# Masking the attention scores on VectorE and taking the exponential on ScalarE in eight pieces with a bias, with the feed-forward loads split up, in a six-layer local-attention megakernel

## The reference

```python
for i in range(DEPTH):                       # 6 layers
    x = attn_layer(shift_tokens(x), Wqkv[i], q_scale[i], k_scale[i], Wo[i]) + x
    x = ffn_layer(shift_tokens(x), ln_g[i], ln_b[i], W1[i], b1[i], W2[i], b2[i]) + x
# local_attention: 16 heads of 64, windows of 32 queries that see 64 keys
    mask = (it < jb) | (it > jb + w) | (jb == -1)
    sim = jnp.einsum('bhwie,bhwje->bhwij', bq, bk2) * QK_SCALE
    sim = jnp.where(mask, -jnp.finfo(sim.dtype).max, sim)
    attn = jax.nn.softmax(sim, -1)
    out = jnp.einsum('bhwij,bhwje->bhwie', attn, bv2)
# ffn_layer: layer norm with gain g and shift bln, then
    hg = xn @ W1 + b1
    a, gate = jnp.split(hg, 2, -1)
    return a * jax.nn.gelu(gate, approximate=False) @ W2 + b2
```

## Time and profile before

| | |
|---|---|
| time, median of 3 runs | 1740.41 us (1739.14 to 1745.62) |
| the profiled execution's own time | 1741.98 us |
| its span in the trace | 1740.2 us |
| mean granted clock of TensorE | 0.985 |
| busy, PE / PEld | 1666.1 us (96%) / 1210.5 us (70%) |
| busy, DVE | 1381.5 us (79%) |
| busy, POOL | 1187.3 us (68%) |
| busy, ACT | 1092.9 us (63%) |

### The profile page before, as it was taken

One profiled execution on the slowest core, in us unless ns is written; L12 is line 12 of the kernel. 1 busy time (PEld: TensorE's weight loads), 2 busy tenths in 40 slices (PEclk: granted clock), 3 DMA queues, 4 the chain that ended last, 5 costly groups with the idle time before them and its releaser, 6 DMA issues.

```text
span 1740.2 us, 74075 instructions
## 1 busy us (share of the span) xinstructions
PE 1666.1 (96%) x31420; PEld 1210.5 (70%) x31420; DVE 1381.5 (79%) x2661; ACT 1092.9 (63%) x1943; POOL 1187.3 (68%) x1163
## 2 busy tenths in 40 slices
PE   5889999999999999999999999999999999999995
PEld 2357777777777777677777677777677777677774
DVE  4688888887888888788888788888788887788863
ACT  2256666666666666566666566666666666566653
POOL 0377777776777767676776677677677777666751
PEclk9799999999999999999999999999999999999998
DMA  3032223332223323222323222333222332222222
GB/s 106 25 93 66 68 67 79 89 76 71 66 68 81 88 68 78 68 65 69 96 71 78 70 68 63 92 78 77 71 69 66 80 87 74 74 64 66 66 61 76
DMA packets 109735, 127.86 MB, mean 73 GB/s; under 512 B 52064, under 2 KB 55648, under 8 KB 109152
## 3 DMA queue, kind: packets, MB, share of 16 engines
q1 hardware_dynamic: 109408, 123.13, 27.9%
HBM read 20.27 MB, written 2.10 MB: 13 GB/s over the span
## 4 chain that ended last, share of the span: by engine, by line
PE 89%; DVE 4%; SPq 2%; ACT 2%; DMA 2%; issue 1%; POOL 0%; ACTq 0%; DVEq 0%; POOLq 0%
PE QKb L471 21%; PE O L594 11%; PE F L499 9%; PE VTb L512 9%; PE S L471 9%; PE S L529 8%; PE S L559 5%; PE F L616 4%; PE F L628 4%; PE F L629 3%; PE S L522 2%; SPq L397 1%; DVE t L823 1%; PE F L568 1%; DMA prm<-in_params 1%
## 5 line engine op out<-in xcount | busy, mean ns | idle before, releaser
L968 POOL TENSOR_TENSOR t<-t 128x512 f32<-128x512 f32 x384 | 488.7, 1273 | 306.6 <-DVE t L823 298.7
L823 DVE TENSOR_TENSOR t<-QKb,table 128x1024 f32<-128x1024 f32 x384 | 468.8, 1221 | 156.8 <-ACT sq L668 156.3
L962 POOL TENSOR_TENSOR t<-t,rn 128x512 f32<-128x512 f32 x384 | 400.5, 1043 | 136.0 <-DVE rn L863 136.0
L471 PE MATMUL QKb<-wq_sb,x_sh 128*128 128x512 f32 x768 | 426.3, 637 | 12.4 <-DVE t L823 11.7
L668 ACT ACTIVATE sq<-QKb 128x512 f32<-128x512 f32 x384 | 230.8, 601 | 321.7 <-PE QKb L471 314.7
L499 PEld LDWEIGHTS F<-wo_sb,OT 128*128 128x128 f32 x1536 | 202.9, 193 | 89.6 <-issue 88.7
L512 PEld LDWEIGHTS VTb<-cst,t 128*128 128x128 f32 x1536 | 186.6, 141 | 104.8 <-issue 94.0
L512 PE MATMUL VTb<-cst,t 128*128 128x128 f32 x1536 | 230.6, 273 | 0.6 <-POOL t L962 0.5
L594 PEld LDWEIGHTS O<-PT,V 64*64 64x64 f32 x12288 | 199.2, 135 | 42.7 <-issue 41.8
L876 DVE TENSOR_REDUCE ss<-sq 128x16 f32<-128x1024 f32 x192 | 224.4, 1169 | 0.0
L594 PE MATMUL O<-PT,V 64*64 64x32 f32 x12288 | 219.2, 221 | 0.9 <-DVE rn L863 0.5
(11 more groups left out here) (136 smaller groups left out, 2165.9 us busy)
## 6 DMA issues: line engine op xcount, KB each, us to landing
V<-v_tok SPq DMA_DIRECT2D x1440, 64.0 KB, 2.0
wq_sb<-in_wqkv SPq DMA_DIRECT2D x36, 256.0 KB, 3.7
wo_sb<-in_wo SPq DMA_DIRECT2D x6, 512.0 KB, 5.0
xs<-xm SPq DMA_DIRECT2D x48, 64.0 KB
xs<-xm SPq DMA_DIRECT2D x48, 63.5 KB
w_sb<-in_w SPq DMA_DIRECT2D x6, 341.0 KB, 3.3
w_sb<-in_w SPq DMA_DIRECT2D x6, 192.0 KB, 3.1
y_spill<-OT SPq DMA_DIRECT2D x1, 1024.0 KB, 4.1
```

The lines of the kernel that those rows point to most:

```text
L471: return pe.matmul(out_, x_sh[:, pr, P * tile:P * (tile + 1)], wq_sb[:, col:col + 512], start=True, stop=True)
L823: dve.tensor_tensor(t12[:, v, :, :].rearrange("p c (h d) -> p c h d", h=8), QK_ps.rearrange("p (h d) -> p h d", h=8).unsqueeze(1) .to_broa ...
L962: pool.tensor_tensor(w, w, rn[:, vv // 4, 8 * (vv % 4):8 * (vv % 4 + 1)].unsqueeze(2) .to_broadcast([P, 8, DH]), ALU.mult).then_inc(qk_nor ...
L968: pool.tensor_tensor(w, w, t12[:, v, 1, :].rearrange("p (h c d) -> p h c d", h=8, c=2)[:, :, ::-1, :], ALU.add).then_inc(add_done, 1)
```

## The change

The mask is no longer a product. The score products start their banks afresh, and DVE adds the mask from `cst` while it moves the scores from PSUM to `E` (this frees the score banks, `mask_done`), and then takes the negated maximum of each group of 64 from `E` (`nmx`). ACT applies that maximum as the bias of the exponential; since a bias is one number per partition, the one instruction of 128x512 becomes eight of 128x64. The two bf16 copies of identity and mask at the start are gone.

`w1`, `w2` and `prm` have a semaphore each. `prm` has two buffers and is loaded a layer ahead; `w1` is loaded when its last product is issued, `w2` likewise. The value projection stands two slots earlier (`L_V` = 4), the token shift one slot later (`F_SH` = 25), the normalisation on POOL one slot later (`F_NM` = 28). And the pieces stand in another order within a slot on every engine.

```diff
-L_V = 6
+L_V = 4
-F_WO, F_MID, F_SH, F_ST, F_NM, F_XT, F_AFF = 21, 24, 24, 27, 27, 29, 29
+F_WO, F_MID, F_SH, F_ST, F_NM, F_XT, F_AFF = 21, 24, 25, 27, 28, 29, 29
...
-                if slot == F_END + 1:
-
-                    wait(sp, ff_final, l * B)
-                    sp.dma_start(w1_sb[:, :], w1[l]).then_inc(in_ffn, 16)
-                    sp.dma_start(w2_sb[:, :, :], w2[l])\
-                      .then_inc(in_ffn, 16)
-                    sp.dma_start(prm[:, :], params[l]).then_inc(in_ffn, 16)
+                if slot == 2:
+
+                    wait(sp, ff_final, (l - 1) * B)
+                    sp.dma_start(prm[:, l % 2, :], params[l]).then_inc(in_prm, 16)
+                if slot == F_HID + 1:
+
+                    wait(sp, w1_ready, l * B * NCH)
+                    sp.dma_start(w1_sb[:, :], w1[l]).then_inc(in_w1, 16)
+                if slot == F_W2 + 1:
+
+                    wait(sp, w2_ready, l * B)
+                    sp.dma_start(w2_sb[:, :, :], w2[l]).then_inc(in_w2, 16)
...
-                        for p in range(2):
-                            pe.matmul(S2[:, p, 0:4 * KEYS], ident_bf[:, :], mask_bf[:, :], start=True, stop=False,
-                                      skip_group_check=True)
...
-                        wait(act, sub_done, a + 1)
-                        act.activation(E[:, k, :], E[:, k, :], ACT.Exp).then_inc(exp_done, 1)
+                        wait(act, max_done, a + 1)
+                        for i in range(8):
+                            w = E[:, k, KEYS * i:KEYS * (i + 1)]
+                            ex = act.activation(w, w, ACT.Exp, bias=nmx[:, k, i:i + 1])
+                        ex.then_inc(exp_done, 1)
...
-                        mv_ = mx[:, k, :].rearrange("p (b c) -> p b c", b=2)
-                        dve.tensor_reduce(mv_, Sv, AX_X, ALU.max).then_inc(max_done, 1)
-                        wait(dve, max_done, a + 1)
+                        Ek = E[:, k, :].rearrange("p (c b k) -> p b c k", c=4, b=2)
                         wait(dve, pt_ready, a - 3)
...
-                        dve.tensor_tensor(E[:, k, :].rearrange("p (c b k) -> p b c k", c=4, b=2), Sv,
-                                          mv_.unsqueeze(3).to_broadcast([P, 2, 4, KEYS]),
-                                          ALU.subtract).then_inc(sub_done, 1)
+                        dve.tensor_tensor(Ek, Sv, cst[:, C_MASK:C_MASK + 4 * KEYS]
+                                          .rearrange("p (c k) -> p c k", k=KEYS).unsqueeze(1)
+                                          .to_broadcast([P, 2, 4, KEYS]), ALU.add).then_inc(mask_done, 1)
+                        wait(dve, mask_done, a + 1)
+                        wait(dve, exp_done, a - 3)
+                        dve.tensor_reduce(nmx[:, k, :], E[:, k, :].rearrange("p (c k) -> p c k", k=KEYS), AX_X, ALU.max,
+                                          negate=True).then_inc(max_done, 1)
```

More of the change, by code:

```diff
@@ L551, in step @@
                         mm.then_inc(tx_ready, 1)
-                    a, k, st, pr = quad(s, par, v, L_PT)
-                    if live(a, QUADS):
-                        wait(pe, p_norm, a + 1)
-                        wait(pe, sub_done, upto(a + 2, QUADS))
-                        wait(pe, pt_evac, a)
-                        for ct in range(4):
-                            mm = pe.transpose(PT_ps[:, P * ct:P * (ct + 1)], E[:, k, P * ct:P * (ct + 1)], ident)
-                        mm.then_inc(pt_ready, 1)
+                    u, vv, st, pr = unit(s, par, v, L_V)
+                    if live(u, UNITS) and vv % 2 == 0:
+                        c = vv // 2
+                        if vv < 4 and pr == 0:
+                            wait(pe, in_v[c], 16 * (st // B + 1))
+                        wait(pe, v_evac, v_units(st, vv, 0) - 1)
+                        wait(pe, mask_done, s_units(s, v))
+                        project(V_ps, pr, c // 2, V_COLS[c % 2]).then_inc(v_ready, 1)
+                    recurrence(in_fill(s, v, 1))
+                    f, pr = batch(s, par, v, F_HID)
+                    if f is not None:
+                        ff_w1(f, pr, [2])
                     f, pr = batch(s, par, v, F_XT)
@@ L698, in step @@
                         stage(BANK_TX[:, 0:N], 1 - par)
+                    f, pr = batch(s, par, v, F_GEL)
+                    if f is not None:
+                        gelus(f, pr, [0, 1])
+                    f, pr = batch(s, par, v, F_HID)
+                    if f is not None:
+                        gelus(f, pr, [2])
                     a, k, st, pr = quad(s, par, v, L_PT)
@@ L703, in step @@
                         act.copy(PT[:, k % 2, :, :].rearrange("p c q -> p (c q)"), PT_ps).then_inc(pt_evac, 1)
-                    f, pr = batch(s, par, v, F_HID)
-                    if f is not None:
-                        gelus(f, pr, [2])
                     f, pr = batch(s, par, v, F_AFF)
                     if f is not None:
-                        if pr == 0:
-                            wait(act, in_ffn, (f // B + 1) * 48)
+                        if f % B == 0:
+                            wait(act, in_prm, (f // B + 1) * 16)
                         wait(act, xnT_ready, f + 1)
                         wait(act, w1_ready, f * NCH)
-                        act.activation(xc[:, :], BANK_XT[:, 0:N], ACT.Identity, bias=prm[:, R_B:R_B + 1],
-                                       scale=prm[:, R_G:R_G + 1]).then_inc(xn_done, 1)
+                        act.activation(xc[:, :], BANK_XT[:, 0:N], ACT.Identity, bias=prm[:, f // B % 2, R_B:R_B + 1],
+                                       scale=prm[:, f // B % 2, R_G:R_G + 1]).then_inc(xn_done, 1)
                     a, k, st, pr = quad(s, par, v, L_PV)
@@ L726, in gelus @@
                     act.activation(hid[0:w, r_, :], BANK_W1[r_][0:w, N:2 * N], ACT.Gelu,
[L727 removed]
+                                   bias=prm[0:w, f // B % 2, R_B1G + r_:R_B1G + r_ + 1]).then_inc(gel_done, 1)
             all_steps(act, step)
@@ L829, in step @@
                     recurrence(in_fill(s, v, 1))
+                    u, vv, st, pr = unit(s, par, v, L_SS)
+                    if live(u, UNITS) and vv % 2 == 0:
+                        wait(dve, sq_done, u + 2)
+                        dve.tensor_reduce(ss[:, vv // 4, 8 * (vv % 4):8 * (vv % 4) + 16],
+                                          sq[:, vv % 4:vv % 4 + 2, :].rearrange("p a (h d) -> p (a h) d", h=8),
+                                          AX_X, ALU.add).then_inc(ss_done, 1)
                     a, k, st, pr = quad(s, par, v, L_S)
```

190 lines of the change are left out of this document (87 added, 103 removed).

## The result

The change makes the kernel slower: 1771.03 us, the median of four runs (1767.88 to 1773.87), against 1740.86 for the kernel before beside it; the ratio is 1.0168, 95% interval 1.0142 to 1.0195. The profiled execution has a span of 1766.1 us (1740.2 before). The forecast was 1746, the range 1712 to 1778: the time is inside the range, and 25 us above the forecast.

What follows compares the result with a forecast made beforehand. PE's own work was taken as the bound, plus stops at layer ends. 43 steps of +0.57 us (-0.85 +0.82 +0.50 +0.10) give +25, layer ends -21, filling and draining +2: +6 in all, so 1746 us, range 1712 to 1778.

Steps and rivals of the forecast that it cites:

- What bounds the kernel: Whole kernel before: PE's own work sets the 33.35 us step; the layer ends cost 21 us more.
- The layer ends, the load half: Layer ends: with prm, w1 and w2 loaded earlier, ACT's wait for parameters and the slow clock go, 21 us.
- The layer ends, the queue half: SP's queue: the shift lands about 2 us ahead of the statistics, costing nothing unless the queue grows.
- The eight exponentials: ACT, each quad: 0.24 us per exponential, 1.92 for eight where one took 0.54; some 265 us in all.
- The two waits of v2 and v3: PE waits 0.82 us for the Newton steps in v2, 0.50 for ACT's weight copy in v3 (score product at 9.70).
- the second rival: Exponentials take 0.18 us or less, only the Newton wait stays, step as before, layer ends gained: 1719 us; chance 0.22.
- In v6, v7, v0 and v1 PE has more to do and I find no wait: Slots v6 to v1 of each step: no wait of PE forecast.
- PE waits for the multiply with the table in more slots than v6 (ACT is the bound): Sign that the prediction is wrong: PE held by this multiply beyond v6, so ACT is the bound.
- The mask product: PE, four quads a step: dropping it saves 0.21 us each, 0.85 a step, 36 us over 43 steps.
- Filling and draining: Short slots at start and end, exponentials of a few quads on the path: 0 to 7 us, 2 taken.
- The fourth: ACT sets the pace of pairs of slots if an exponential exceeds 0.24 us: 1777 at 0.27, some 1840 at 0.34; chance 0.22.
- The fifth: Layer ends give nothing, as SP's fuller queue in v0 to v2 brings wq, shift or w1 late: 1767 us; chance 0.08.

Runs made afterwards that it cites:

- experiment 1: Kernel before with only the feed-forward loads split up (own semaphores, two prm buffers, w1 and w2 loaded earlier): 1720.06 us.
- experiment 6: Kernel after with the value projection back in its old slots (L_V = 6), the shift still in v1: 1759.07 us.
- experiment 3: Kernel after with the old mask product, maximum, subtraction and single exponential put back; order, constants and loads as changed: 1770.76 us.
- 4: Kernel after with one 128x512 exponential without bias in place of the eight, the maximum not subtracted: 1753.99 us.
- experiment 9: Kernel after with the value projection in its old slots and four 128x128 exponentials, two groups sharing the first one's maximum: 1713.62 us.
- 11: Kernel before, in its order and constants, with the arithmetic and the loads of the change: 1757.08 us.
- 2: Kernel before with only the arithmetic of the change (no mask product, eight exponentials with bias), old order and loads: 1789.95 us.
- Experiment 7: Kernel after with the shift a slot earlier (v0) and the Newton steps' scratch in SBUF instead of bank O: 1773.61 us.
- experiment 10: Kernel after with the arithmetic of before put back and the value projection in its old slots: 1736.56 us.
- experiment 12: Kernel before with the loads split up and the Newton steps' scratch in SBUF, nothing else of the change: 1725.65 us.

## Why the prediction was right and wrong

**What bounds the kernel: right.** PE's own work was the period, and the layer ends cost 21 us: experiment 1 takes them away and leaves the step alone.

**The layer ends, the load half: right.** 21 us forecast, 21 measured by the cut in experiment 1. One detail of the text is wrong: `w1` and `w2` leave four and two slots earlier (34 and 36 against 38), not five and seven; nothing hung on it.

**The layer ends, the queue half: this is the step that failed in kind.** I wrote that the shift lands "about 2 us ahead of the statistics that read it; it costs nothing unless the queue grows". In an ordinary step the count holds: the shift is handed over 3.0 us ahead of the statistics. But the queue did grow. The first move of a step waits on SP for the value product of v6, 325 us in all, and what stands behind it (the next moves, `wq`, the shift) leaves late; at a layer end five loads of `wq` stand in the same queue, and there the shift lands after the statistics could start. That is 13.5 us over in the 43 steps, 12.7 of them at the layer ends, and 12.7 go with `L_V` = 6 (experiment 6), as do 4.4 in the draining (that kernel's filling is 2.9 longer). I had argued that moves which must wait anyway start where they did, which the traces bear out (440.50 after, 440.93 in experiment 6), and left out that they hold up the queue behind them. In kernels with a faster step it is worse: 24.4 us over in experiment 3, 37.3 in 4.

**The eight exponentials: right.** 0.24 us from the engine each, from the gelus' pitch: the eight take 1.92 to the next start. The rule that I set beside it, the Trainium skill's page "ScalarE: Activation LUTs", section "What ACT_TABLE_LOAD costs", on what an activation costs with a bias (240 ns each by the fixed part less the overlap), agrees with the trace, and experiment 9 agrees with its width term: twice the columns add 54 ns (0.84 a column). That ACT sets the long step is shown by experiments 4 and 9, where the number of exponentials alone takes the step from 34.11 to 33.27 (4 against the kernel after, where the bias goes too; 9 against 6). In 11 and 2 the old order gives 34.14.

**The two waits of v2 and v3: right in place and, together, in size; the price of the first by itself is wrong.** 32.6 us for the Newton steps (35 forecast) and 14.1 for the copy of the weights (20 forecast); v1 to v4 is 11.93 us in most steps (11.94 forecast) and v4 to v6 7.36 (7.35). But the terms 0.82 and 0.50 can't be taken away one by one. The moment 9.70 came from ACT's chain alone, and no Newton step is in it. Experiment 7 takes the wait for the Newton steps away: the stretch stays at 11.93, and PE waits for ACT's copies instead. Experiments 4 and 9 shorten ACT's chain and leave that wait: 11.39. So in the kernel after ACT's chain is the longer by 0.54, all of the wait for the Newton steps lies in its shadow, and it comes out only when ACT is faster. This is also the second rival's case, exponentials cheap enough that only the wait for the Newton steps stays: it gave the step of before, 33.35, and 33.27 came.

**"In v6, v7, v0 and v1 PE has more to do and I find no wait": wrong.** By the step of 33.92 this stretch should take 14.63 us, 0.10 less than before; it takes 14.82, so the term is mis-sized by 0.2 us a step, 8 us in 43 steps (34.11, not 33.92). The timeline of that stretch shows one place where PE is held, the projection of v0:

```profile
1058.28 2.01 ACT L676 ACTIVATE E<-E,nmx 128x64 f32<-128x64 f32 x8
...
1062.88 0.62 ACT L670 ACTIVATE sq<-QKb 128x512 f32<-128x512 f32 x1
...
1063.53 1.23 DVE L826 TENSOR_TENSOR t<-QKb,table 128x1024 f32<-128x1024 f32 x1 [0.84 <-ACT sq L670]
...
1064.90 1.10 PE L474 MATMUL QKb<-wq_sb,x_sh 128*128 128x512 f32 x2
```

The projection starts 0.14 us behind the multiply's end (1063.53 + 1.23), the multiply waits for the squares, and these stand on ACT behind the exponentials of v6, four copies and two staging copies. With four exponentials the stretch is 14.68, so 0.14 of the 0.2 is the eight exponentials. The other 0.05 comes with the order: with the old arithmetic in that order the stretch is 14.79, against 14.73 before, though neither the mask nor the exponential changed. And it is not v0 alone: in 32 or more of 36 middle steps the projections of v0, v2, v4 and v6 start 0.05 to 0.15 us behind the multiply's end. With four exponentials the ties of v4 and v6 are gone and that of v0 stays: there the order alone, with two copies on ACT ahead of the squares of v7, is enough. "PE waits for the multiply with the table in more slots than v6 (ACT is the bound)" was one of the prediction's own signs of being wrong, and it was met.

**The mask product: about two thirds of it comes.** Once ACT is out of the way, the new arithmetic in the new order saves 0.55 a step (33.82 in experiment 10, 33.27 in 9), not 0.85; the wait for the Newton steps, which PE now reaches earlier, grows from 26.3 to 31.8 us and takes 0.1 of the missing 0.3; where the rest goes was not settled. The row in experiment 9:

```profile
PE O L588 <- DVE rn L892: 31.8, 47, 1.0
```

The busy time of PE was a poor thing to check it by. I forecast 36 us less; it fell by 23 in the kernel after. But experiments 6 and 9 have the same 31036 products in the same order and count 1644.1 and 1620.0 us. The one with more waits counts more; the ends of matmuls in a profile are modelled, which may be why.

**Filling and draining: mis-sized.** 2 us taken, 8.6 measured (2.7 and 5.9). Draining falls from 121.2 to 116.8 with the late value projection, so 4.4 of its 5.9 are the queue again. The filling differs by up to 8 us between the kernels (159.8 to 167.7) in a way that I did not settle.

**The sum.** +25 for the steps became +33, -21 for the layers' ends became -15, +2 became +9: +26 instead of +6. The sign of the forecast for the steady step was right. Of the 20 us between +6 and +26, about 8 are in the step, 6 at the layer ends and 7 in filling and draining, all to the slow side. Two rivals happened in part. The fourth's condition did not come, since the exponential is not above 0.24, but its consequence did, small: ACT sets the pace of more pairs of slots than v4 and v5. The fifth came for a quarter of its size: SP's queue brings the shift late at the layer ends, and 6 of their 21 us are lost. I had given 0.40 to a time above 1749.1.

**What beats both kernels.** Experiment 1, the loads alone, which computes just what the kernel before does: 1720.06. Experiment 9: 1713.62; a softmax is the same whatever one number is subtracted in a group, but the first group's maximum guards the second against large exponents only where the two are of like size. Four exponentials in the order of before were not tried. That order costs 0.47 a step less with the old arithmetic, so this would be the next kernel to run.

## What to carry to other kernels

An instruction that is cut in eight keeps its fixed part eight times: 336 ns for 64 columns, 390 for 128 and 626 for 512 here, and the number of instructions counts for more than the columns; look for a bias that more columns can share. Work that moves from the bounding engine to one with room "on average" pays only where its new chain is not on the path: ACT had 26% idle after, and yet set the step. A transfer issued early whose buffer is not free is worse than one issued late, because it holds an in-order queue; moving the victim only picks another victim. And a change in several parts should be timed part by part, as the best of them here was hidden by the others, and the parts did not add up.

## What the runs showed of the hardware that I had not expected

- DVE's small operation of 128x32 takes 0.17 us in some slots and 1.17 in others when it writes to SBUF (605 ns in the mean), and 183 ns in the mean when it writes to PSUM. Only the place of the scratch was changed. The long ones, 46 in experiment 12 and 43 in 7, all end 0.04 us behind the POOL instruction that was running as they began: the trace books this wait as DVE's busy time, and no view of waits shows it.
- SP needs 0.62 us to issue one of the 64 KB moves (7 in 4.35 us, in experiment 6), and 2.6 to 2.8 us for the third DMA of the shift, one row of 64 numbers. With some 30 moves a step, these issue times alone take 18 us or more of SP's 34.
- The granted clock did not fall in the new waits of some tenths of a microsecond in each step: it is 1.00 in every window from 200 to 1600 us, and its mean is 0.992 (0.985 before, where it fell behind stops such as that of the earlier trace rows).
